# Attention on one core: one comparison row moved from VectorE to ScalarE, a subtraction moved from GpSimd to VectorE, GpSimd's sums at another place, and TensorE's loop written out

## The chip, the cores and the metric

The kernel runs on one core of a Trainium2 chip. The metric is the device time of one execution in microseconds (us). The core's engines work side by side and meet at semaphores: TensorE (PE in the profile; its weight loads are PEld), VectorE (DVE), ScalarE (ACT), GpSimd (POOL) and SyncE (SP), which here only issues DMAs.

## The reference

`x` is 2048 rows of 512 numbers, `adj` a 2048 x 2048 matrix of zeros and ones. A graph attention layer with 16 heads of 32 columns is followed by an expert layer; the change touches the first alone.

```python
seq = (layernorm(x) @ W_seq).reshape(N, H, DH)          # N = 2048, H = 16, DH = 32
scores = score1[:, :, None] + score2[:, None, :]        # seq . a1 and seq . a2, for each head
scores = leaky_relu(scores, 0.2)
scores = scores + (1.0 - adj)[None, :, :] * MASK_VAL    # -65500
attn = softmax(scores, axis=-1)
hidden = einsum('hij,jhd->ihd', attn, seq).reshape(N, 512)
x = x + elu(hidden @ W_out + b_out)
x = x + expert_layer(layernorm(x))
```

## The kernel before, in words

The exponential of a leaky ReLU of a sum is one of two products, chosen by the sign of score1 + score2. So the kernel builds no softmax matrix. For each head it builds a matrix of zeros and ones, "is the sum positive", masks it with `adj`, and multiplies it with a value matrix that holds both products for each of the 2048 columns; a second matrix product with `adj` itself supplies the part of the other sign. Both are scaled for each row and added.

**Units.** The work is cut into 32 units: 8 pairs of heads `p`, and in each pair four units `k` = 0 to 3, where `k // 2` is the head of the pair and `k % 2` the half of the 2048 output rows (1024 of them). I number units u = 4p + k, from 0 to 31. A unit's mask matrix `m8[:, k]` has 16 rows (blocks `j` of 128 columns of the reference's matrix), each of 128 partitions x 1024 bytes. `DVE_J` of the 16 rows are compared on VectorE (`compare`, L653), the others on ScalarE by a steep sigmoid (`compare_rows`, L600). VectorE then masks its own rows (`mask_own`, L661) and those of ScalarE (`mask_acts`, L668) with a bitwise and.

**The value matrix.** `vs[:, b]` holds one head's values as two float16 halves, a high and a low one, whose sum stands for a float32. GpSimd forms four products in `vtmp` (L735 twice, L737 twice), ScalarE rounds them to the high half (`split_high`, L608), and GpSimd subtracts to get the low half (L741). There is one `vtmp`.

**Matmuls.** TensorE runs 256 matmuls for a unit (L791 with 132 columns, L795 with 66), into three PSUM banks; the units alternate between two sets of banks. It starts unit u when its masks are ready (`m_ready`), when the low half is there (`lo_ready`, at even k), and when the sums of unit u-2 have been read out (`sums_ready`).

**VectorE's loop.** The iteration for unit u (28 of them, for u = 0 to 27, in a hardware loop over p) waits until TensorE has finished unit u, reads its sums out of PSUM in three reductions (`collect`, L675), compares the rows of unit u+4, masks its own rows of unit u+4, and masks ScalarE's rows of unit u+3. For the last four units only `collect` is left (and one `mask_acts`).

**ScalarE's loop.** When unit u is done it compares its rows of unit u+4; at odd k it first does `split_high` for the next pair.

**GpSimd's loop.** `combine` (L750 twice, L755) scales and adds the sums of unit u as soon as `collect` of u is done; at odd k `build` comes ahead of it: the four products, the wait for ScalarE, the subtraction.

SyncE stages the score rows of unit u+2 by DMA when both compares of unit u are done (L558). All loops over p are hardware loops, TensorE's too (L778).

Of the kernel before, what the change touches and what calls it, by code (L numbers as in the profile page):

```python
# [30 lines left out]
ALU = mybir.AluOpType  # L31
# [11 lines left out]
WD = 2 * W1  # L43
# [4 lines left out]
MB = 4  # L48
AB = 3
UNITS = H * NIC  # L50
DVE_J = 7
E, LAT, INTER, SH = 8, 256, 256, 2048
TC = 512
NC_ = N // TC
# [12 lines left out]
def build(nc, x, adjT, w_seq, a_cols, a_mask, w_out, b_out, gateT, corr, w1T, w2T, fc1T, fc2T, upT, downT,  # L67
# [6 lines left out]
    with ctx:  # L74
        def sem(name):
            return ctx.enter_context(nc.semaphore(name))
# [34 lines left out]
        vs = at(O_VS, 2112, f16).rearrange("p (b j c) -> p b j c", b=2, j=T)  # L111
# [429 lines left out]


        PAIRS = H // 2
        prod_ready, hi_copied, lo_ready, vtmp_free = sem("prod_ready"), sem("hi_copied"), sem("lo_ready"), sem("vtmp_free")
        dve_compared, act_compared, own_masked = sem("dve_compared"), sem("act_compared"), sem("own_masked")
        m_ready, unit_in_psum, sums_ready, sums_free = sem("m_ready"), sem("unit_in_psum"), sem("sums_ready"), sem("sums_free")
        act_passed, pe_passed = sem("act_passed"), sem("pe_passed")
        bias_copied, scaled_step = sem("bias_copied"), sem("scaled_step")

        GROUPS = [(0, 3), (3, 3), (6, 2)]  # L550
# [2 lines left out]
        with nc.Block() as block:  # L553
# [93 lines left out]
            def _(dve):  # L647
# [23 lines left out]
                def collect(p, k):  # L671
# [5 lines left out]
                            bank[3 * (k % 2) + g][:, 0:n * WV].rearrange("p (t s c) -> p t c s", t=n, s=2), AX.X)  # L677
                    last.then_inc(sums_ready, 1)

                def split_low():  # L680

                    dve.wait_ge(wo_high, 1)
                    nc.vector.tensor_tensor(wo_parts[:, 1, :, :], wo_sb, wo_parts[:, 0, :, :].bitcast(f32), ALU.subtract)
                    nc.vector.tensor_tensor(bout_parts[0:1, 1, :], bout_sb[0:1, :], bout_parts[0:1, 0, :].bitcast(f32),
                                            ALU.subtract)
                    nc.vector.tensor_scalar(ones_r[0:1, :], ident2[0:1, :], 0.0, 1.0, ALU.mult, ALU.add).then_inc(wo_low, 1)

                def body(p, last):
                    for k in range(4):
                        if last and k == 3:  # L690
                            split_low()
                        dve.wait_ge(unit_in_psum, 4 * p + k + 1)
                        collect(p, k)
                        if not last:
                            compare(p + 1, k)
                            mask_own(p + 1, k)

                        if k == 0:
                            mask_acts(p, 3)
                        elif not last:  # L700
                            mask_acts(p + 1, k - 1)
# [10 lines left out]
                apply_empty_rows((2, 3))  # L712
                dve.wait_ge(seq_in_psum, T)
                compare(0, 1)
                mask_own(0, 1)
                mask_acts(0, 1)
                compare(0, 2)
                mask_own(0, 2)
                compare(0, 3)
# [6 lines left out]
            @block.gpsimd  # L726
            def _(pool):
                setup_pool(pool)
                def build(p, b):

                    h = 2 * p + b
                    pool.wait_ge(vtmp_free, 2 * p + b + 1)
                    vh = v_sb.rearrange("p t (h d) -> p t h d", h=H)[:, :, h, :]
                    for c, val in enumerate((bval, nval)):
                        nc.gpsimd.tensor_tensor(vtmp[:, :, c * W1:c * W1 + DH], vh,  # L735
                                                val[:, :, bass.ds(h, 1)].to_broadcast([P, T, DH]), ALU.mult)
                        last = nc.gpsimd.tensor_copy(vtmp[:, :, c * W1 + DH:(c + 1) * W1], val[:, :, bass.ds(h, 1)])  # L737
                    last.then_inc(prod_ready, 1)
                    pool.wait_ge(prod_ready, 2 * p + b + 1)
                    pool.wait_ge(hi_copied, 2 * p + b + 1)  # L740
                    nc.gpsimd.tensor_tensor(vs[:, b, :, WD:], vtmp, vs[:, b, :, 0:WD], ALU.subtract).then_inc(lo_ready, 1)  # L741
                    pool.wait_ge(lo_ready, 2 * p + b + 1)
                    pool.sem_inc(vtmp_free, 1)

                def combine(p, k):
                    h = 2 * p + k // 2
# [8 lines left out]
                    nc.gpsimd.tensor_tensor(hid[:, tiles, h, :], scaled[:, k % 2, :, 0:W1],  # L755
                                            scaled[:, k % 2, :, W1:], ALU.add).then_inc(sums_free, 1)

                def body(p, last):
                    for k in range(4):
                        if k % 2 and not last:  # L760
                            pool.wait_ge(unit_in_psum, 4 * p + k + 1)
                            build(p + 1, k // 2)
                        combine(p, k)

                pool.sem_inc(sums_free, 2)
                pool.sem_inc(vtmp_free, 1)
                pool.wait_ge(bn_ready, 1)
                pool.wait_ge(v_copied, T)
                build(0, 0)
                build(0, 1)  # L770
                with pool.Fori(0, PAIRS - 1) as p:
                    body(p, False)
                body(PAIRS - 1, True)

            @block.tensor
            def _(pe):
                setup_pe(pe)
                with pe.Fori(0, PAIRS) as p:  # L778
                    for k in range(4):
                        b = k // 2  # L780
                        if k % 2 == 0:
                            pe.wait_ge(lo_ready, 2 * p + b + 1)
                        pe.wait_ge(sums_ready, 4 * p + k + 1)
                        pe.wait_ge(m_ready, 4 * p + k + 1)
                        pe.sem_inc(pe_passed, 1)
                        for i in range(IT):
                            g, slot = GROUP_OF[i]
                            o = bank[3 * (k % 2) + g][:, slot * WV:(slot + 1) * WV]
# [1010 lines left out]
```

## Time and profile before

| | us |
|---|---|
| three timed runs: median (lowest to highest) | 1131.07 (1130.83 to 1133.75) |
| the profiled execution: its own time | 1135.76 |
| its span, first to last instruction | 1133.9 |
| VectorE busy | 856.1 (75%) |
| TensorE busy | 1042.5 (92%) |
| ScalarE busy | 618.2 (55%) |
| GpSimd busy | 315.0 (28%) |

The stage that the change touches runs from about 110 us to 565 us of the span. Matmuls overlap, so TensorE's busy time isn't its work; starts of groups of matmuls say more. In a row of the timeline the first number is the start, the second the duration; rows of one kind are merged with their count.

### The profile page before, as it was taken

How to read it: one execution, taken by the hardware profiler on the slowest of the kernel's cores; microseconds unless marked ns; L12 is line 12 of the kernel's file. 1: busy time of each engine (PE TensorE's matmuls, PEld its weight loads, DVE VectorE, ACT ScalarE, POOL GpSimd, SP SyncE). 2: the span in 40 equal slices, each digit the busy share in tenths (PEclk: the TensorE clock that was granted, in tenths of full speed). 3: DMA queues.
4: the chain of work that ended last, by engine and by line, in shares of the span. 5: the costliest groups of instructions: out<-in, count | busy, mean ns of one | idle time of the engine just before them, and what ended most of it. 6: DMA issues, size and time to landing. Idle time of an engine off the chain costs nothing. (4 is left out here: it accounts for less than half of the span.)

```text
span 1133.9 us, 27344 instructions
## 1 busy us (share of the span) xinstructions
PE 1042.5 (92%) x11304; PEld 916.3 (81%) x11304; DVE 856.1 (75%) x1216; ACT 618.2 (55%) x939; POOL 315.0 (28%) x287
## 2 busy tenths in 40 slices
PE   5799687989898989978899999999999999999998
PEld 4576587989898989978867788888888887777887
DVE  4756999999999999997359953345876558985554
ACT  2226777777777777773045543334445445664432
POOL 1101434444444445463234200000026300005510
PEclk9899898999898989898989999999999999999999
DMA  8356011111111111153073510002016213444242
GB/s 299 112 192 240 20 58 40 40 40 40 40 46 52 40 40 40 40 168 113 2 285 123 174 58 1 1 1 75 1 48 212 85 42 126 131 130 150 75 141 101
DMA packets 51472, 102.68 MB, mean 91 GB/s; under 512 B 5889, under 2 KB 25985, under 8 KB 48770
## 3 DMA queue, kind: packets, MB, share of 16 engines
q1 hardware_dynamic: 44386, 81.68, 21.2%
q10 hardware_dynamic: 3888, 10.72, 2.6%
q0 software_dynamic: 3072, 8.39, 2.3%
q8 instruction: 105, 1.72, 0.6%
q14 instruction: 21, 0.17, 0.1%
HBM read 74.69 MB, written 26.08 MB: 89 GB/s over the span
## 5 line engine op out<-in xcount | busy, mean ns | idle before, releaser
L791 PE MATMUL bank<-arena 128*128 128x132 f16 x4096 | 298.0, 226 | 52.6 <-issue 43.3
L600 ACT ACTIVATE arena<-arena 128x1024 fp8e4<-128x1024 f32 x288 | 303.2, 1135 | 7.4 <-DMA arena<-s_rows 4.5
L791 PEld LDWEIGHTS bank<-arena 128*128 128x128 fp8e4 x4096 | 256.1, 100 | 56.8 <-issue 56.8
L653 DVE TENSOR_SCALAR arena<-arena 128x1024 uint8<-128x1024 f32 x224 | 205.9, 988 | 0.0
L1170 PE MATMUL bank<-xt,up_parts 128*128 128x512 f32 x768 | 186.3, 391 | 0.0
L1637 PE MATMUL bank<-down_parts,h_parts 128*128 128x512 f32 x768 | 184.5, 389 | 0.1
L795 PE MATMUL bank<-arena 128*128 128x66 f16 x4096 | 179.3, 199 | 0.0
L1637 PEld LDWEIGHTS bank<-down_parts,h_parts 128*128 128x128 f32 x768 | 144.0, 188 | 30.5 <-issue 0.5
L1170 PEld LDWEIGHTS bank<-xt,up_parts 128*128 128x128 f32 x768 | 142.3, 188 | 28.7 <-ACT relu_sb L1119 0.2
L795 PEld LDWEIGHTS bank<-arena 128*128 128x128 fp8e4 x4096 | 160.8, 100 | 0.0
L1144 DVE TENSOR_TENSOR relu_sb<-relu_sb 128x512 f32<-128x512 f32 x64 | 44.3, 692 | 116.9 <-ACT relu_sb L1119 111.7
L750 POOL TENSOR_TENSOR arena<-arena 128x264 f32<-128x264 f32 x64 | 65.2, 1038 | 220.4 <-DVE arena L675 219.6
L1119 ACT ACTIVATE relu_sb<-bank 128x512 f32<-128x512 f32 x64 | 38.3, 598 | 147.3 <-PE bank L1170 140.9
L668 DVE TENSOR_TENSOR arena<-arena 128x2304 uint32<-128x2304 uint32 x32 | 105.5, 3298 | 0.2
L1591 POOL DMA_INDIRECT sorted_latent_rows<-latent,slot_idx x32 | 35.0, 1094 | 208.7 <-DVE slot_idx L1457 190.9
L1159 DVE TENSOR_TENSOR down_parts<-down_sb,down_parts 128x512 fp32r<-128x512 f32 x64 | 44.3, 691 | 51.3 <-ACT down_parts L1138 47.8
L1138 ACT CAST down_parts<-down_sb 128x512 fp32r<-128x512 f32 x64 | 39.9, 623 | 73.8 <-PE bank L1637 70.5
L1603 POOL DMA_INDIRECT y_gathered<-sorted_expert_rows,slot_idx x32 | 32.9, 1028 | 154.5 <-DMA sorted_expert_rows<-expert_y 133.9
L661 DVE TENSOR_TENSOR arena<-arena 128x1792 uint32<-128x1792 uint32 x32 | 67.2, 2101 | 1.1
L608 ACT CAST arena<-arena 128x1056 f16<-128x1056 f32 x16 | 17.2, 1074 | 89.9 <-POOL arena L737 89.9
L675 DVE TENSOR_REDUCE arena<-bank 128x198 f32<-128x396 f32 (+1 forms) x96 | 44.1, 513 | 24.0 <-PE bank L791 24.0
L735 POOL TENSOR_TENSOR arena<-arena 128x512 f32 (+1 forms) x32 | 47.7, 1490 | 28.3 <-ACT arena L209 25.1
(225 smaller groups left out, 1477.8 us busy)
## 6 DMA issues: line engine op xcount, KB each, us to landing
hid<-in_adjT SPq DMA_DIRECT2D x16, 1024.0 KB, 4.9
arena<-s_rows SPq DMA_DIRECT2D x30, 512.0 KB, 3.8
sorted_latent_rows<-zeros SPq DMA_DIRECT2D x1, 4992.0 KB, 18.7
xs<-sorted_latent_rows SPq DMA_DIRECT2D x39, 128.0 KB, 2.2
sorted_expert_rows<-expert_y SPq DMA_DIRECT2D x39, 128.0 KB, 1.7
arena<-in_x SPq DMA_DIRECT2D x4, 1024.0 KB, 12.0
xr<-in_x SPq DMA_DIRECT2D x16, 256.0 KB, 2.8
up_sb<-in_upT ACTq DMA_DIRECT2D x1, 4096.0 KB, 14.7
```

The costliest lines, as they stand in the source:

```text
L600: last = nc.scalar.activation(m8[:, k, j, :], s1b[:, k % 2, :], ACT.Sigmoid, bias=bias_now[:, k // 2, j:j + 1], scale=STEEP, saturate=False)
L653: last = nc.vector.tensor_scalar(mu8[:, k, j, :], s1b[:, k % 2, :], neg_s2[:, 2 * p + k // 2, j:j + 1], float(ONE8), ALU.is_gt, ALU.mult)
L661: nc.vector.tensor_tensor(mw[:, k, 0:DVE_J, :], mw[:, k, 0:DVE_J, :], adjw[:, 0:DVE_J, cols], ALU.bitwise_and).then_inc(own_masked, 1)
L668: nc.vector.tensor_tensor(mw[:, k, DVE_J:, :], mw[:, k, DVE_J:, :], adjw[:, DVE_J:, cols], ALU.bitwise_and).then_inc(m_ready, 1)
L735: nc.gpsimd.tensor_tensor(vtmp[:, :, c * W1:c * W1 + DH], vh, val[:, :, bass.ds(h, 1)].to_broadcast([P, T, DH]), ALU.mult)
L750: last = nc.gpsimd.tensor_tensor(scaled[:, k % 2, :, c * W1:(c + 1) * W1], sums[:, k % 2, :, c * W1:(c + 1) * W1], coef[:, h, tiles, c:c + ...
L791: last = nc.tensor.matmul(o, m8[:, k, j, i * P:(i + 1) * P], vs[:, b, j, :], start=(j == 0), stop=(j == T - 1))
L795: nc.tensor.matmul(od, adj8[:, ja, (k % 2) * IC + i * P:(k % 2) * IC + (i + 1) * P], vs[:, b, ja, :].rearrange("p (s c) -> p s c", s=2)[:, ...
L1144: nc.vector.tensor_tensor(r, r, r, ALU.mult).then_inc(sq_ready, 1)
L1159: nc.vector.tensor_tensor(sb_[:, s % 2, 1, :], down_sb[:, s % FS, :], sb_[:, s % 2, 0, :].bitcast(f32), ALU.subtract).then_inc(b_ready, 1)
L1170: last = nc.tensor.matmul(bank[6 + s % 2][:, :], sa[:, s % 2, a, k, :], xt[c][:, b, k, :], start=(i == 0), stop=(i == len(mm) - 1))
L1637: last = nc.tensor.matmul(ob[t][:, :], hhl[:, s % 2, a, t * P:(t + 1) * P], sb_[:, s % 2, b, :], start=(n == 0 and (a, b) == TERMS[0]), st ...
```

## The change

It does four things.

- `DVE_J` goes from 7 to 6: VectorE compares 6 rows of each unit and ScalarE 10. `mask_own` shrinks from 1792 to 1536 words a partition and `mask_acts` grows from 2304 to 2560.
- The subtraction that gives the low half moves from GpSimd to VectorE (`low_values`), behind the compare at odd k; GpSimd keeps the four products (`products`).
- GpSimd handles unit u-1 (`combine`) in the iteration for u, when `m_ready` has reached u+3 (the last thing in VectorE's iteration before) and TensorE has finished u. The products move from odd k to even k, behind `combine`, with a wait for the low half of the head before. The semaphore `vtmp_free` goes.
- TensorE's loop over the 8 pairs is written out.

```diff
-DVE_J = 7
+DVE_J = 6
@@ VectorE
+                def low_values(p, b):
+                    dve.wait_ge(hi_copied, 2 * p + b + 1)
+                    nc.vector.tensor_tensor(vs[:, b, :, WD:], vtmp, vs[:, b, :, 0:WD], ALU.subtract).then_inc(lo_ready, 1)
...
                             compare(p + 1, k)
+                            if k % 2:
+                                low_values(p + 1, k // 2)
                             mask_own(p + 1, k)
...
                 compare(0, 1)
+                low_values(0, 0)
                 mask_own(0, 1)
                 mask_acts(0, 1)
+                low_values(0, 1)
                 compare(0, 2)
@@ GpSimd
-                def build(p, b):
+                def products(p, b):
...
-                    pool.wait_ge(vtmp_free, 2 * p + b + 1)
...
                     last.then_inc(prod_ready, 1)
-                    pool.wait_ge(prod_ready, 2 * p + b + 1)
-                    pool.wait_ge(hi_copied, 2 * p + b + 1)
-                    nc.gpsimd.tensor_tensor(vs[:, b, :, WD:], vtmp, vs[:, b, :, 0:WD], ALU.subtract).then_inc(lo_ready, 1)
-                    pool.wait_ge(lo_ready, 2 * p + b + 1)
-                    pool.sem_inc(vtmp_free, 1)
...
-                def body(p, last):
+                def body(p, first):
                     for k in range(4):
-                        if k % 2 and not last:
-                            pool.wait_ge(unit_in_psum, 4 * p + k + 1)
-                            build(p + 1, k // 2)
-                        combine(p, k)
+                        pool.wait_ge(m_ready, 4 * p + k + 3)
+                        pool.wait_ge(unit_in_psum, 4 * p + k + 1)
+                        if k or not first:
+                            combine(p - (k == 0), (k - 1) % 4)
+                        if k % 2 == 0:
+                            pool.wait_ge(lo_ready, 2 * (p + 1) + k // 2)
+                            products(p + 1, k // 2)
...
-                build(0, 0)
-                build(0, 1)
-                with pool.Fori(0, PAIRS - 1) as p:
+                products(0, 0)
+                pool.wait_ge(lo_ready, 1)
+                products(0, 1)
+                body(0, True)
+                with pool.Fori(1, PAIRS - 1) as p:
                     body(p, False)
-                body(PAIRS - 1, True)
+                combine(PAIRS - 2, 3)
+                for k in range(4):
+                    combine(PAIRS - 1, k)
@@ TensorE
-                with pe.Fori(0, PAIRS) as p:
+                for p in range(PAIRS):
```

**VectorE, ahead of its loop.** The rows are the last work before the first `collect`; L682 is `low_values`, and `hi_copied` is what ScalarE's `split_high` raises.

```order
 L653 TENSOR_SCALAR arena<-arena 128x1024 [waits s1_staged_hi,seq_in_psum,dve_step]
-L653 TENSOR_SCALAR arena<-arena 128x1024 x6
-L661 TENSOR_TENSOR arena<-arena 128x1792 [waits dve_compared]
-L668 TENSOR_TENSOR arena<-arena 128x2304 [waits own_masked,act_compared]
+L653 TENSOR_SCALAR arena<-arena 128x1024 x5
+L682 TENSOR_TENSOR arena<-arena 128x16x66 [waits hi_copied]
+L661 TENSOR_TENSOR arena<-arena 128x1536 [waits dve_compared]
+L668 TENSOR_TENSOR arena<-arena 128x2560 [waits own_masked,act_compared]
+L682 TENSOR_TENSOR arena<-arena 128x16x66 [waits hi_copied]
 L653 TENSOR_SCALAR arena<-arena 128x1024 [waits s1_staged_lo]
```

The two subtractions of the first pair of heads now stand in VectorE's queue, the second one ahead of the compare of unit 2.

**VectorE, an iteration at odd k in its loop.** The rows run from the last reduction of `collect` to the mask of ScalarE's rows.

```order
 L675 TENSOR_REDUCE arena<-bank 128x132
 L653 TENSOR_SCALAR arena<-arena 128x1024 [waits s1_staged_hi]
-L653 TENSOR_SCALAR arena<-arena 128x1024 x6
+L653 TENSOR_SCALAR arena<-arena 128x1024 x5
+L681 REGISTER_ALU
+L682 TENSOR_TENSOR arena<-arena 128x16x66 [waits hi_copied]
 L660 REGISTER_ALU
-L661 TENSOR_TENSOR arena<-arena 128x1792 [waits dve_compared]
-L668 TENSOR_TENSOR arena<-arena 128x2304 [waits own_masked,act_compared]
```

One comparison is gone and one subtraction of 16 x 66 elements has come, between the compare and `mask_own`.

**GpSimd, in its loop.** First the kernel before, from the products of one head to the `combine` behind them.

```order
-L732 REGISTER_ALU [waits unit_in_psum]
-L735 ISA [waits vtmp_free]
-L735 REGISTER_ALU
-L735 TENSOR_TENSOR arena<-arena 128x16x32
-L737 COPY arena<-arena 128x16
-L735 ISA
-L735 TENSOR_TENSOR arena<-arena 128x16x32
-L737 COPY arena<-arena 128x16
-L741 TENSOR_TENSOR arena<-arena 128x16x66 [waits hi_copied,prod_ready]
-L748 REGISTER_ALU [waits lo_ready]
-L750 ISA [waits sums_ready]
```

Now the changed kernel, where `combine` is L752 and L757, and the products are L742 and L744.

```order
+L752 ISA [waits sums_ready,unit_in_psum,m_ready]
+L752 TENSOR_TENSOR arena<-arena 128x8x33
+L752 ISA
+L752 TENSOR_TENSOR arena<-arena 128x8x33
+L757 ISA [waits scaled_step]
+L757 TENSOR_TENSOR hid<-arena 128x8x33
+L767 REGISTER_ALU
+L742 ISA [waits lo_ready]
+L742 REGISTER_ALU
+L742 TENSOR_TENSOR arena<-arena 128x16x32
+L744 COPY arena<-arena 128x16
```

The wait for ScalarE in the middle of GpSimd's work is gone, and `combine` stands ahead of the products behind a wait for VectorE's last mask.

## Rows read from the trace of the kernel before

**Rows 1.** Windows: VectorE's 28 iterations, then the tail; PEclk is the granted clock.

```profile
155.37:527.93 372.56, 332.29 (x6921) 328.90 (x6922) 371.60 (x338) 273.33 (x273) 178.22 (x154) 0.93 0.16 53
528.00:562.00 34.00, 34.00 (x759) 34.00 (x756) 10.37 (x14) 2.42 (x2) 10.32 (x9) 1.00 0.16 52
```

**Rows 2.** Timeline of VectorE over two iterations in the middle of its loop.

```profile
304.53 1.37 DVE L675 TENSOR_REDUCE arena<-bank 128x198 f32<-128x396 f32 x3
305.82 5.88 DVE L653 TENSOR_SCALAR arena<-arena 128x1024 uint8<-128x1024 f32 x7
...
313.68 2.55 DVE L668 TENSOR_TENSOR arena<-arena 128x2304 uint32<-128x2304 uint32 x1
316.14 1.38 DVE L675 TENSOR_REDUCE arena<-bank 128x198 f32<-128x396 f32 x3
317.44 7.51 DVE L653 TENSOR_SCALAR arena<-arena 128x1024 uint8<-128x1024 f32 x7
324.99 2.02 DVE L661 TENSOR_TENSOR arena<-arena 128x1792 uint32<-128x1792 uint32 x1
326.93 4.46 DVE L668 TENSOR_TENSOR arena<-arena 128x2304 uint32<-128x2304 uint32 x1
331.32 1.37 DVE L675 TENSOR_REDUCE arena<-bank 128x198 f32<-128x396 f32 x3
```

**Rows 3.** Timeline of GpSimd over the same stretch.

```profile
306.09 2.02 POOL L750 TENSOR_TENSOR arena<-arena 128x264 f32<-128x264 f32 x2 [3.90 <-DVE arena L675]
...
317.74 1.99 POOL L750 TENSOR_TENSOR arena<-arena 128x264 f32<-128x264 f32 x2 [8.57 <-DVE arena L675]
...
326.35 2.63 POOL L741 TENSOR_TENSOR arena<-arena 128x1056 f16<-128x1056 f32 x1 [1.33 <-ACT arena L608]
```

**Rows 4.** Timeline of VectorE ahead of its loop.

```profile
113.37 3.35 DVE L397 TENSOR_TENSOR arena<-arena 128x2048 uint32<-128x2048 uint32 x1
...
123.69 2.29 DVE L397 TENSOR_TENSOR arena<-arena 128x2048 uint32<-128x2048 uint32 x1
...
130.13 4.73 DVE L653 TENSOR_SCALAR arena<-arena 128x1024 uint8<-128x1024 f32 x7
...
155.37 1.38 DVE L675 TENSOR_REDUCE arena<-bank 128x198 f32<-128x396 f32 x3
```

**Rows 5.** Timeline, 435 to 438 us: a GpSimd subtraction beside `collect`.

```profile
435.53 3.06 POOL L741 TENSOR_TENSOR arena<-arena 128x1056 f16<-128x1056 f32 x1 [1.33 <-ACT arena L608]
436.54 1.37 DVE L675 TENSOR_REDUCE arena<-bank 128x198 f32<-128x396 f32 x3
```

**Rows 6.** Timeline of GpSimd in the tail, where VectorE is idle.

```profile
540.81 1.24 POOL L750 TENSOR_TENSOR arena<-arena 128x264 f32<-128x264 f32 x2 [7.22 <-DVE arena L675]
```

**Rows 7.** Timeline of ScalarE: split, nine compares, and the copy of the biases.

```profile
325.12 1.07 ACT L608 CAST arena<-arena 128x1056 f16<-128x1056 f32 x1 [6.22 <-POOL arena L737]
326.10 9.46 ACT L600 ACTIVATE arena<-arena 128x1024 fp8e4<-128x1024 f32 x9
335.46 0.19 ACT L592 COPY arena<-arena 128x16 f32 x1
```

**Rows 8.** Waits, 85 to 560 us: total, times, longest.

```profile
ACT arena L608 <- POOL arena L737: 89.9, 16, 7.2
PEld bank L791 <- issue: 56.8, 22, 6.9
```

**Rows 9.** Timeline of TensorE: start of unit 0, then of unit 28 with a second stall.

```profile
123.15 0.27 PE L791 MATMUL bank<-arena 128*128 128x132 f16 x1 [6.47 <-issue]
...
509.95 0.27 PE L791 MATMUL bank<-arena 128*128 128x132 f16 x1 [5.82 <-issue]
...
516.03 0.73 PE L791 MATMUL bank<-arena 128*128 128x132 f16 x5 [3.69 <-issue]
```

**Rows 10.** Timeline of VectorE: `collect` of unit 28 and of unit 31.

```profile
527.93 1.38 DVE L675 TENSOR_REDUCE arena<-bank 128x198 f32<-128x396 f32 x3
...
562.38 1.39 DVE L675 TENSOR_REDUCE arena<-bank 128x198 f32<-128x396 f32 x3 [6.31 <-PE bank L791]
```

More of the change, by code:

```diff
@@ L543, in build @@
         PAIRS = H // 2
-        prod_ready, hi_copied, lo_ready, vtmp_free = sem("prod_ready"), sem("hi_copied"), sem("lo_ready"), sem("vtmp_free")
+        prod_ready, hi_copied, lo_ready = sem("prod_ready"), sem("hi_copied"), sem("lo_ready")
         dve_compared, act_compared, own_masked = sem("dve_compared"), sem("act_compared"), sem("own_masked")
         m_ready, unit_in_psum, sums_ready, sums_free = sem("m_ready"), sem("unit_in_psum"), sem("sums_ready"), sem("sums_free")
-        act_passed, pe_passed = sem("act_passed"), sem("pe_passed")
+        act_passed = sem("act_passed")
         bias_copied, scaled_step = sem("bias_copied"), sem("scaled_step")
@@ L756, in combine @@
                                             scaled[:, k % 2, :, W1:], ALU.add).then_inc(sums_free, 1)
-                def body(p, last):
+                def body(p, first):
                     for k in range(4):
-                        if k % 2 and not last:
-                            pool.wait_ge(unit_in_psum, 4 * p + k + 1)
-                            build(p + 1, k // 2)
-                        combine(p, k)
+                        pool.wait_ge(m_ready, 4 * p + k + 3)
[5 more added lines that the diff above has]
+                            products(p + 1, k // 2)
                 pool.sem_inc(sums_free, 2)
-                pool.sem_inc(vtmp_free, 1)
                 pool.wait_ge(bn_ready, 1)
                 pool.wait_ge(v_copied, T)
-                build(0, 0)
-                build(0, 1)
-                with pool.Fori(0, PAIRS - 1) as p:
+                products(0, 0)
[3 more added lines that the diff above has]
+                with pool.Fori(1, PAIRS - 1) as p:
                     body(p, False)
-                body(PAIRS - 1, True)
+                combine(PAIRS - 2, 3)
+                for k in range(4):
+                    combine(PAIRS - 1, k)
             @block.tensor
@@ L784, in _ @@
                         pe.wait_ge(m_ready, 4 * p + k + 1)
-                        pe.sem_inc(pe_passed, 1)
                         for i in range(IT):
```

## The prediction

> **What bounds the kernel now.** I read the windows first, to find the engine without idle time. Over VectorE's 28 iterations, 155.4 to 527.9 us, it is busy 371.6 of 372.6 us; ScalarE is busy 273, GpSimd 178 [rows 1]. TensorE shows 332, but its matmuls overlap. Its real need is read where nothing holds it up: in the tail it runs 759 matmuls in 34.0 us, so a unit of 256 takes 11.5 us [rows 1]. The loop takes 372.6 / 28 = 13.3 us a unit. So VectorE sets the pace there, and TensorE is 1.8 us a unit ahead of it.
>
> The timeline of VectorE shows what a unit costs. Two neighbouring iterations take 11.6 us (304.5 to 316.1) and 15.2 us (316.1 to 331.3), 26.8 for both [rows 2]. They do the same work. The difference is in two places: the seven compares take 5.88 us in the one and 7.51 in the other, and the mask of ScalarE's rows 2.55 and 4.46. The timeline of GpSimd says why [rows 3]: in both, `combine` starts right behind `collect`, beside the compares; in the second the four products follow it; and the 2.63 us subtraction (326.35) lies on the slow mask. Ahead of the loop, where GpSimd is idle, the same seven compares take 4.73 us [rows 4]. So GpSimd's work costs VectorE 1.15 us for each `combine` (5.88 - 4.73), 1.63 for a head's products (7.51 - 5.88), and 1.91 for the subtraction: 5.84 in two iterations of 26.8.
>
> After the last compare the bound changes. From the `collect` of unit 28 to that of unit 31 there are 34.45 us [rows 10], three units of TensorE at 11.5. TensorE should have been further ahead, since two sets of banks let it be. But it started unit 28 at 509.95 after 5.8 us without a releaser and stood still again for 3.7 us [rows 9]. Such stalls sum to 56.8 us in 22 places [rows 8]; the large ones that I show follow the loop's jump back.
>
> **The change, part by part.**
>
> *VectorE's own work.* I count from start to start, without GpSimd, for two iterations. `collect` is 1.30 (316.14 to 317.44) [rows 2]. A compare row is 4.73 / 7 = 0.68, so six are 4.1. `mask_own` is 1.94 to the next start for 1792 words; between 2.02 us for 1792 and 2.55 for 2304 lies 1.03 ns a word [rows 2], so 1536 words are 1.68. `mask_acts` goes from 2.47 to 2.73. That is 9.8 us an iteration. `low_values` has no row on VectorE. By the same 1.03 ns an element, 1056 elements cost about 1.2 us; the bounds are nothing and GpSimd's 2.63 for the same subtraction [rows 3]. I take 1.2, because VectorE's own two-input rows are nearest. It comes in one iteration of two: 20.8 us for two iterations, where the old work alone is 21.0. So one compare is traded for half a subtraction, and almost the whole gain must come from the other 5.84 us.
>
> *GpSimd beside VectorE.* The 1.91 of the subtraction goes. `combine` now starts with `collect`, not behind it. Does it cost anything there? Once in the trace a GpSimd subtraction (435.53 to 438.6) lies right over a `collect`, which took 1.37 us, as everywhere [rows 5]. So a `combine` in that place costs nothing. Alone, its first two operations take 1.24 us [rows 6], about the 1.30 of `collect`; the third falls on the compares, a third of 1.15, 0.39. The products stay beside the compares: 1.63 for two iterations. Together 1.63 + 2 x 0.39 = 2.4, and 0.14 for a late start of GpSimd, since its sequencer has register work first (my estimate). Two iterations cost 20.8 + 2.5 = 23.3 us, or 11.65 a unit. If nothing of `combine` were hidden, it would be 20.8 + 1.63 + 2.3 = 24.7, or 12.35 a unit.
>
> The Trainium skill ("SBUF — State Buffer", Who interferes with whom) has `tensor_reduce` never in contention with GpSimd, and the trace agrees (1.37 us). The same section calls the shared port pair an exclusive lock, held for the whole instruction. By that rule VectorE would lose the full time of each GpSimd operation, some 12.2 us a unit and 15 us more in all by my estimate; the trace doesn't agree, since a `combine` of 1.9 us alone costs 1.15.
>
> *The other engines at that pace.* ScalarE's nine compares take 9.36 us from start to start; ten take 10.4, and two units with one split (0.98) and the copy of the biases with its wait (0.4) 22.2 us, or 11.1 a unit [rows 7]. Today the split waits on GpSimd's products, 89.9 us in 16 times [rows 8], because both start at the same signal. Now the products are made one iteration earlier, so ScalarE finds them. TensorE needs 11.5. So three engines stand at 11.1, 11.5 and 11.65. VectorE remains the last, by little; as TensorE may be up to two units ahead, unequal iterations even out.
>
> *TensorE's loop written out* removes the jumps. In the loop VectorE's 1.8 us a unit hid their stalls; now that cover is 0.15 us, so this edit is what lets the others count. It gains by itself only in the tail. There, `collect` of unit 28 is followed by 1.4 us and two units of 11.5, 24.4 us to the `collect` of unit 31 instead of 34.45: -10.0.
>
> *The start.* This is the one place that gets worse. TensorE started unit 0 at 123.15 [rows 9]. Now the low half of head 0 comes from VectorE, behind the compare of unit 1 that started at 130.13 [rows 4]. With GpSimd idle the instructions ahead of it shorten: one `L397` took 3.35 beside GpSimd and 2.29 alone, and I count four such pieces, 3.7 us with the missing compare not counted. So the compare starts at 126.4, the low half is ready at 126.4 + 4.1 + 1.2 = 131.7, and TensorE starts 8.5 us later. It has slack: VectorE wants unit 1 only in its second iteration. What is queued behind VectorE's second `low_values` matters more: GpSimd's products of head 1 begin at 131.7 and take some 7 us beside the masks, ScalarE's split is done at about 139.7, the low half at 140.9. Then VectorE has two compares, two `mask_own` and one `mask_acts`, 14.3 us, and reaches its first `collect` at 155.2, where it is now (155.37). ScalarE, held at that same split, has its rows of unit 3 at about 161; VectorE wants them at about 163. I add 0.5 us for a wait for the second split.
>
> *The sum.* The 28 iterations: 28 x 11.65 = 326.2 for 372.6, -46.4. Start: -0.2 + 0.5. Tail: -10.0. Total -56 us. The profiled execution took 1135.8 us, for a span of 1133.9, so the same execution would take 1079.7. The median of the timed runs is 4.7 below that execution, so by it 1075. I say 1077. The expert layer behind is started by TensorE's and VectorE's last unit and moves as a whole.
>
> **The rivals.**
>
> *GpSimd's cost stays, or the clock does.* If `combine` isn't hidden, or starts late, 12.35 a unit instead of 11.65 is 28 x 0.7 = 20 us: 1097. The clock gives the same sum. In the loop the mean granted clock is 0.93 of 2.4 GHz, 1.00 in the tail [rows 1]. If short gaps between units kept it at 0.93, a unit would take 11.5 / 0.93 = 12.4. Against it: with 0.15 us of idle a unit there should be hardly a gap.
>
> *TensorE stalls in straight code too.* Without the first, the stalls are some 50 us for 28 units [rows 8], 1.8 a unit. If they belonged to the amount of instructions and not to the jump, TensorE would need 11.5 + 1.8 = 13.3 us and nothing would be gained: 1131. Against it speaks that 34 us of the tail went without one [rows 1]. The Trainium skill ("Runtime: NRT & Kernel Launch", Instruction fetch mechanics) says that a taken branch breaks the sequential prefetch; the stall at 509.95, at the top of the loop's body, agrees.
>
> *Slower: ScalarE becomes the bound.* It has 1.1 us to spare in two units. If GpSimd, now behind two more waits, made the products late for the split, ScalarE would wait there, VectorE's `low_values` with it, and everything behind that in VectorE's queue. At the longest wait of today, 7.2 us [rows 8], two units cost 29.4: 14 x 2.6 = 36 us more, 10 less in the tail, 1157. It beats the old 26.8 from a wait of 4.6 us on. Against it: the products have a whole iteration.
>
> *TensorE is the bound.* Should VectorE need under 11.5, the unit stays there: 28 x 0.15 = 4 us less, 1073, and with a better start a few more.
>
> **How the numbers follow.** The forecast (1067 to 1090) has 0.64, GpSimd's cost or the clock (1091 to 1104) 0.24, TensorE at its bound with a start so much better that it ends below 1067 0.04, stalls in straight code 0.05, ScalarE 0.03. A price of 2.63 for `low_values` would give 28 x 0.7 = 20 us more, 1097 too. The range of 1066 to 1100 leaves out somewhat under 2 in 10. A difference of 0.3%, 3.4 us, is about what a measurement of this kernel tells from none. Faster 0.92, same 0.05, slower 0.03.
>
> **What the changed profile would show.** The start of one `collect` to the one after the next should be 23.3 us, with compares of 4.1 to 4.5 us at odd k and about 6.1 at even k, `mask_acts` never above 2.9, `low_values` 1.2 to 1.3. TensorE should start unit 0 near 131.7 and show no stalls at the heads of pairs. The first `collect` should start near 155 and the last near 506. I am wrong if six compares still take over 5.2 us at odd k, if the split waits for GpSimd in the loop, or if TensorE has idle time without a releaser.

## The result and the profile after

The changed kernel takes 1078.18 us (median of four runs, 1076.02 to 1079.98) where the kernel before takes 1132.41 (1130.83 to 1133.92). The ratio is 0.9525, with a 95% interval of 0.9501 to 0.9548: 4.75% faster, 54 us. The prediction was 1077.

The profiled execution of the changed kernel took 1076.02 us for a span of 1074.2. Its windows over VectorE's 28 iterations and over the tail answer to [rows 1]; the columns are the same.

```profile
152.90:479.68 326.78, 324.60 (x7174) 322.67 (x7170) 325.20 (x323) 313.84 (x314) 119.16 (x140) 1.00 0.20 67
480.00:505.00 25.00, 25.00 (x556) 25.00 (x554) 10.29 (x13) 2.42 (x2) 10.54 (x9) 1.00 0.01 3
```

The 28 iterations take 326.8 us instead of 372.6, or 11.67 a unit. VectorE is still busy all the time, but now TensorE and ScalarE are too: 325, 325 and 314 us of 327. The granted clock is 1.00 where it was 0.93. The timeline of VectorE over two iterations answers to [rows 2].

```profile
269.13 1.38 DVE L675 TENSOR_REDUCE arena<-bank 128x198 f32<-128x396 f32 x3
270.43 6.09 DVE L653 TENSOR_SCALAR arena<-arena 128x1024 uint8<-128x1024 f32 x6
276.55 1.76 DVE L661 TENSOR_TENSOR arena<-arena 128x1536 uint32<-128x1536 uint32 x1
278.23 2.82 DVE L668 TENSOR_TENSOR arena<-arena 128x2560 uint32<-128x2560 uint32 x1
280.96 1.38 DVE L675 TENSOR_REDUCE arena<-bank 128x198 f32<-128x396 f32 x3
282.26 4.50 DVE L653 TENSOR_SCALAR arena<-arena 128x1024 uint8<-128x1024 f32 x6
286.67 1.25 DVE L682 TENSOR_TENSOR arena<-arena 128x1056 f16<-128x1056 f32 x1
287.84 1.75 DVE L661 TENSOR_TENSOR arena<-arena 128x1536 uint32<-128x1536 uint32 x1
289.51 2.82 DVE L668 TENSOR_TENSOR arena<-arena 128x2560 uint32<-128x2560 uint32 x1
```

From 269.13 to 280.96 to 292.25 are 11.83 and 11.29 us, 23.1 for both; the two iterations behind them take 23.5, and 23.3 is the mean. In the loop the masks are 1.76 and 2.82 everywhere, with nothing beside them. Only the compares still vary, 6.09 with GpSimd's products and 4.50 without; in every second pair of iterations they are 6.30 and 4.63. There `combine` starts 0.46 and 0.42 us behind the start of `collect`, not 0.26 and 0.30, and its second operation reaches further into the compares. GpSimd's timeline over the same stretch answers to [rows 3].

```profile
269.39 1.24 POOL L752 TENSOR_TENSOR arena<-arena 128x264 f32<-128x264 f32 x2 [8.95 <-DVE arena L668]
270.81 0.87 POOL L757 TENSOR_TENSOR hid<-arena 128x264 f32 x1 [0.18 <-POOL arena L752]
271.64 1.52 POOL L742 TENSOR_TENSOR arena<-arena 128x512 f32 x1
273.11 0.67 POOL L744 COPY arena<-arena 128x16 f32 x1
```

The first two operations of `combine` lie beside `collect`, at the 1.24 us that they take alone [rows 6], and `collect` keeps its 1.38 us. They were 2.02 beside the compares.

Ahead of the loop, the timeline of VectorE answers to [rows 4]; the second row is `low_values` of head 0, the fourth that of head 1, the last that of head 2 in the second iteration, and a bracket is the idle time ahead.

```profile
107.74 0.69 DVE L395 TENSOR_SCALAR arena<-bank 128x512 uint8<-128x512 f32 x1 [5.01 <-PE bank L460]
...
128.53 1.25 DVE L682 TENSOR_TENSOR arena<-arena 128x1056 f16<-128x1056 f32 x1
...
131.55 3.51 DVE L668 TENSOR_TENSOR arena<-arena 128x2560 uint32<-128x2560 uint32 x1
137.45 1.26 DVE L682 TENSOR_TENSOR arena<-arena 128x1056 f16<-128x1056 f32 x1 [2.39 <-ACT arena L608]
...
144.39 4.06 DVE L653 TENSOR_SCALAR arena<-arena 128x1024 uint8<-128x1024 f32 x6
...
152.90 1.38 DVE L675 TENSOR_REDUCE arena<-bank 128x198 f32<-128x396 f32 x3
...
170.38 1.26 DVE L682 TENSOR_TENSOR arena<-arena 128x1056 f16<-128x1056 f32 x1 [1.10 <-ACT arena L608]
```

TensorE starts unit 0 right behind the first `low_values`, later than in [rows 9], and the `collect` of units 28 and 31 stand at 479.68 and 505.33 where [rows 10] had them at 527.93 and 562.38. First TensorE's timeline, then VectorE's.

```profile
129.83 0.29 PE L798 MATMUL bank<-arena 128*128 128x132 f16 x1 [15.01 <-DVE arena L682]
...
476.82 0.24 PE L802 MATMUL bank<-arena 128*128 128x66 f16 x2 [0.54 <-issue]
```

```profile
479.68 1.37 DVE L675 TENSOR_REDUCE arena<-bank 128x198 f32<-128x396 f32 x3
...
505.33 1.39 DVE L675 TENSOR_REDUCE arena<-bank 128x198 f32<-128x396 f32 x3 [6.31 <-PE bank L798]
```

### The profile page after: what moved, and what is told of

Read it like the earlier page. It is cut to its first block, busy times and chain, and to the rows that moved or that the text cites. A ratio compares the mean times of both kernels' runs of the same rounds, so it can differ in the third digit from the quotient of the medians.

```text
span 1074.2 us, 27252 instructions
## 1 busy us (share of the span) xinstructions
PE 1018.5 (95%) x11304; PEld 894.5 (83%) x11304; DVE 806.5 (75%) x1200; ACT 648.9 (60%) x971; POOL 247.7 (23%) x271
## 4 chain that ended last, share of the span: by engine, by line
PE 47%; DVE 2%; issue 2%; DMA 1%; POOL 0%; ACT 0%; SPq 0%; POOLq 0%; DVEq 0%; ACTq 0%
PE bank L1177 16%; PE bank L1644 16%; PE bank L1009 3%; PE bank L1721 2%; PE bank L1672 1%; PE bank L1673 1%; PE bank L1675 1%; DMA xs<-sorted_latent_rows 1%; PE bank L1691 1%; PE bank L1665 1%; PE bank L1629 1%; PE bank L1006 1%; PE bank L1627 1%; PE bank L997 1%; PE bank L1018 1%
## 5 line engine op out<-in xcount | busy, mean ns | idle before, releaser
L600 ACT ACTIVATE arena<-arena 128x1024 fp8e4<-128x1024 f32 x320 | 336.4, 1135 | 3.0 <-ACT arena L592 3.0
L798 PE MATMUL bank<-arena 128*128 128x132 f16 x4096 | 283.8, 221 | 15.6 <-DVE arena L682 15.0
L798 PEld LDWEIGHTS bank<-arena 128*128 128x128 fp8e4 x4096 | 245.0, 97 | 17.7 <-DVE arena L682 15.5
L802 PE MATMUL bank<-arena 128*128 128x66 f16 x4096 | 172.6, 195 | 1.6 <-issue 1.6
L653 DVE TENSOR_SCALAR arena<-arena 128x1024 uint8<-128x1024 f32 x192 | 166.4, 933 | 0.0
L802 PEld LDWEIGHTS bank<-arena 128*128 128x128 fp8e4 x4096 | 153.7, 98 | 1.9 <-issue 1.9
L752 POOL TENSOR_TENSOR arena<-arena 128x264 f32<-128x264 f32 x64 | 45.4, 731 | 218.9 <-DVE arena L668 195.9
L668 DVE TENSOR_TENSOR arena<-arena 128x2560 uint32<-128x2560 uint32 x32 | 90.8, 2838 | 0.2
L1598 POOL DMA_INDIRECT sorted_latent_rows<-latent,slot_idx x32 | 34.7, 1085 | 209.0 <-DVE slot_idx L1464 191.0
L742 POOL TENSOR_TENSOR arena<-arena 128x512 f32 (+1 forms) x32 | 48.6, 1520 | 63.2 <-ACT arena L209 25.1
L661 DVE TENSOR_TENSOR arena<-arena 128x1536 uint32<-128x1536 uint32 x32 | 56.1, 1753 | 0.6
L1009 PE MATMUL bank<-wo_parts,hT 128*128 128x512 f32 x192 | 49.7, 409 | 0.0
```

Source lines behind the costliest of these rows:

```text
L600: last = nc.scalar.activation(m8[:, k, j, :], s1b[:, k % 2, :], ACT.Sigmoid, bias=bias_now[:, k // 2, j:j + 1], scale=STEEP, saturate=False)
L653: last = nc.vector.tensor_scalar(mu8[:, k, j, :], s1b[:, k % 2, :], neg_s2[:, 2 * p + k // 2, j:j + 1], float(ONE8), ALU.is_gt, ALU.mult)
L661: nc.vector.tensor_tensor(mw[:, k, 0:DVE_J, :], mw[:, k, 0:DVE_J, :], adjw[:, 0:DVE_J, cols], ALU.bitwise_and).then_inc(own_masked, 1)
L668: nc.vector.tensor_tensor(mw[:, k, DVE_J:, :], mw[:, k, DVE_J:, :], adjw[:, DVE_J:, cols], ALU.bitwise_and).then_inc(m_ready, 1)
L752: last = nc.gpsimd.tensor_tensor(scaled[:, k % 2, :, c * W1:(c + 1) * W1], sums[:, k % 2, :, c * W1:(c + 1) * W1], coef[:, h, tiles, c:c + ...
L798: last = nc.tensor.matmul(o, m8[:, k, j, i * P:(i + 1) * P], vs[:, b, j, :], start=(j == 0), stop=(j == T - 1))
```

## The experiments

Eight kernels were run, and the changed one again as a reference. Ratios are to the kernel before, measured on the same chip. The first three undo one part of the change each, the fourth does one part alone.

### TensorE's loop as a hardware loop again

```diff
-                for p in range(PAIRS):
+                with pe.Fori(0, PAIRS) as p:
...
                         pe.wait_ge(m_ready, 4 * p + k + 1)
+                        pe.sem_inc(pe_passed, 1)
```

The semaphore increment stood in the loop of the kernel before too, and went with it. It stands ahead of all four units of a turn.

> The changed kernel with TensorE's loop over the head pairs as a hardware loop again (and its semaphore increment before each unit). Theory: the stalls behind each jump cost TensorE about 1.8 us a unit, and now nothing covers them, so a unit takes 11.5 + 1.8 = 13.3 us instead of 11.65, 28 units give +46 us, and the stall at unit 28 another 10: 1078 becomes about 1125 to 1134, nearly the whole gain gone. Rival A: writing out the loop is worth only the tail's 10 us, 1088. Rival B: VectorE's waits cover part of the stalls in the loop, as its own pace is 11.65: 1100 to 1115.

Measured: 1126.0 us, ratio 0.9952 (0.9935 to 0.9969). Of 54 us only 6 are left. TensorE's timeline in this kernel shows the start of the loop's body in two neighbouring turns.

```profile
394.47 0.22 PE L799 MATMUL bank<-arena 128*128 128x132 f16 x1 [2.78 <-DVE arena L675]
397.02 0.73 PE L799 MATMUL bank<-arena 128*128 128x132 f16 x5 [1.19 <-issue]
446.47 0.22 PE L799 MATMUL bank<-arena 128*128 128x132 f16 x1 [3.14 <-issue]
449.50 0.73 PE L799 MATMUL bank<-arena 128*128 128x132 f16 x5 [1.56 <-issue]
```

The bracket of the first row names VectorE, that of the third, at the same place one turn later, nobody. Such gaps stand in the first unit of a turn alone, not at its other three, so they belong to the jump and not to the increment. VectorE's waits in this kernel show who is late:

```profile
DVE arena L675 <- PE bank L799: 60.3, 9, 10.1
```

VectorE, almost without idle time in the loop of both main kernels, waits 60.3 us in nine places for TensorE: six are at the head of a turn, three in the tail, where the changed kernel waits too. This turn is 52 us (394.5 to 446.5), 13.0 a unit. So the stalls of the jump are real time for TensorE, some 6 us a turn with the lower granted clock (0.93 over the loop, where the changed kernel has 1.00), and the first theory stands, with 1.5 us a unit and not the 1.8 that it took. Rivals A and B fall.

### `combine` behind its own `collect` again

```diff
                     for k in range(4):
-                        pool.wait_ge(m_ready, 4 * p + k + 3)
-                        pool.wait_ge(unit_in_psum, 4 * p + k + 1)
-                        if k or not first:
-                            combine(p - (k == 0), (k - 1) % 4)
+                        combine(p, k)
                         if k % 2 == 0:
```

> The changed kernel with GpSimd's combine of unit u right behind collect of unit u again, in the same iteration (products still at even k behind it). Theory: three GpSimd operations lie beside the compares and cost VectorE 1.15 us an iteration instead of about 0.45: 28 x 0.7 = +20 us, 1098, with six compares at odd k near 5.2 us. Rival: the place doesn't matter, because TensorE at 11.5 us a unit is nearly the bound and collect loses as much as the compares gain: 1078 within 4 us.

Measured: 1096.02 us, ratio 0.9681 (0.9654 to 0.9708): 18 us more than the changed kernel. VectorE's timeline:

```profile
301.12 6.04 DVE L653 TENSOR_SCALAR arena<-arena 128x1024 uint8<-128x1024 f32 x6
307.19 2.51 DVE L661 TENSOR_TENSOR arena<-arena 128x1536 uint32<-128x1536 uint32 x1
...
313.68 5.21 DVE L653 TENSOR_SCALAR arena<-arena 128x1024 uint8<-128x1024 f32 x6
```

At odd k the compares take 5.21 us, as said; at even k the work that no longer fits beside them has moved on to `mask_own`, 2.51 instead of 1.76. Two iterations take 24.5 us (299.83 to 324.38). That is 0.6 us an iteration for three operations beside the compares instead of one.

### The subtraction on GpSimd again, beside the compares

```diff
                         if k % 2 == 0:
                             pool.wait_ge(lo_ready, 2 * (p + 1) + k // 2)
                             products(p + 1, k // 2)
+                        else:
+                            low_pool(p + 1, k // 2)
@@ VectorE
-                            if k % 2:
-                                low_values(p + 1, k // 2)
```

> The changed kernel with the subtraction of the low half on GpSimd again, but behind combine at odd k, so beside the compares and mask_own and not on mask_acts. Theory (what matters is which VectorE instruction GpSimd's work lies on): two iterations lose VectorE's 1.2 us and gain 0.4 to 1.9 us of collisions, a difference of -0.8 to +0.7 us for two iterations, 14 x that is -11 to +10 us, but TensorE's 11.5 us a unit lets no more than 4 us be gained: 1074 to 1088. The nearest row for a collision with compares says 0.4 us for each us of GpSimd, 2.63 us give 1.05: 1076. Rival (the move to VectorE is itself the gain, since the subtraction costs 1.9 us wherever it stands on GpSimd): 1088. TensorE starts unit 0 some 9 us earlier, which should not show in the end.

Measured: 1087.64 us, ratio 0.9607 (0.9582 to 0.9631): 9.5 us more than the changed kernel. Here the theory falls and the rival holds. The timelines of VectorE and of GpSimd at odd k:

```profile
333.55 6.36 DVE L653 TENSOR_SCALAR arena<-arena 128x1024 uint8<-128x1024 f32 x6
```

```profile
310.03 0.87 POOL L753 TENSOR_TENSOR hid<-arena 128x264 f32 x1 [0.19 <-POOL arena L748]
310.87 2.56 POOL L759 TENSOR_TENSOR arena<-arena 128x1056 f16<-128x1056 f32 x1
```

Six compares take 6.36 us beside the subtraction and 4.50 without: it costs VectorE 1.86 us, as it did on the mask (1.91), and not the 1.05 that I had worked out from `combine`. On VectorE itself it adds 1.05: in the changed kernel, with GpSimd idle, the compares and `low_values` take 5.15 us up to `mask_own` (124.54 to 129.69), the compares alone 4.10 (144.39 to 148.49). The difference of 0.81 us is 11.3 over 14 pairs of iterations, and VectorE's wait of 1.1 us in the second iteration (170.38) is gone. That makes 10.2, and the 28 iterations of the two profiles differ by 10.3 (337.05 and 326.78). TensorE started unit 0 at 123.18 here, 6.6 us earlier than in the changed kernel, and had to wait for VectorE all the same.

### The kernel before, with TensorE's loop written out

```diff
-                with pe.Fori(0, PAIRS) as p:
+                for p in range(PAIRS):
```

> The kernel before with TensorE's loop written out and nothing else. Theory: in the loop VectorE sets the pace at 13.3 us a unit and hides TensorE's stalls, so only the tail gains: 10 us, 1122 for 1132. Rival: TensorE's stalls held VectorE up somewhere too, or its lower clock did: more than 15 us gained, below 1117.

Measured: 1128.72 us, ratio 0.9963 (0.9948 to 0.9978): 3 us gained (2 to 6 by the interval), fewer than the 10 expected, and the rival is out. The tail did shrink: from the `collect` of unit 28 to that of unit 31 it is 25.1 us (530.80 to 555.90) instead of 34.45. But the 28 iterations ahead of it are longer, 375.2 us instead of 372.6. In the kernel before TensorE's stalls had twice shifted GpSimd's products, so that the subtraction began behind the start of the mask, and not ahead of it. VectorE's timeline of the kernel before at one such place, then of this one at the same place:

```profile
434.06 2.56 DVE L668 TENSOR_TENSOR arena<-arena 128x2304 uint32<-128x2304 uint32 x1
```

```profile
434.40 4.47 DVE L668 TENSOR_TENSOR arena<-arena 128x2304 uint32<-128x2304 uint32 x1
```

In the kernel before, the subtraction ran from 435.53 [rows 5], on the end of the mask and over `collect`, and the two iterations took 25.4 us (423.33 to 448.75). Without the stalls all pairs of iterations take 26.8. So over a quarter of the tail's gain, 2.6 of 9.4 us, was given back in the loop. That leaves 6.8 us of gain by the two traces, where the medians differ by 3.2; why stays open.

### Seven rows, and five, on VectorE

```diff
-DVE_J = 6
+DVE_J = 7
```

> The changed kernel with seven compare rows of a unit on VectorE and nine on ScalarE, as before the change. Theory: VectorE is the last of three engines by 0.15 us a unit, so one more row of 0.68 us counts in full: 28 x 0.68 = +19 us, 1097. Rival: TensorE or ScalarE really sets the pace at 11.6 us and part of the row is hidden: less than 12 us more, under 1090.

Measured: 1099.97 us, ratio 0.9697 (0.9675 to 0.972). By the ratios, 0.9697 against 0.9525, it is 19.5 us slower than the changed kernel. VectorE's two iterations take 24.4 and 24.8 us in turn, 24.6 in the mean, where 23.3 + 2 x 0.68 = 24.7 was expected. The row counts in full. With five rows:

```diff
-DVE_J = 6
+DVE_J = 5
```

> The changed kernel with five compare rows on VectorE and eleven on ScalarE. Theory: ScalarE needs 22.2 us for two units and 1.04 us more for each row, 24.3, so 12.15 us a unit, above TensorE's 11.5 and VectorE's 11.0; ScalarE sets the pace and VectorE waits at the mask of ScalarE's rows: 28 x 0.5 = +14 us, 1092. Rival: ScalarE's slack between its units is more than I read, and TensorE's 11.5 is the floor: 1074.

Measured: 1095.28 us, ratio 0.9664 (0.9648 to 0.968), by the ratios 15.7 us slower than the changed kernel. ScalarE's timeline:

```profile
295.00 1.06 ACT L608 CAST arena<-arena 128x1056 f16<-128x1056 f32 x1
295.97 11.54 ACT L600 ACTIVATE arena<-arena 128x1024 fp8e4<-128x1024 f32 x11
307.41 0.19 ACT L592 COPY arena<-arena 128x16 f32 x1
307.81 11.55 ACT L600 ACTIVATE arena<-arena 128x1024 fp8e4<-128x1024 f32 x11 [0.21 <-ACT arena L592]
319.27 1.06 ACT L608 CAST arena<-arena 128x1056 f16<-128x1056 f32 x1
```

No idle time but the 0.21 of the bias copy, and 24.3 us from split to split (295.00 to 319.27), as expected. VectorE waits, though not where I had said: it waits at `low_values` for the split, 34.7 us in 15 places, and at the mask of ScalarE's rows only 6.7 us in three.

```profile
DVE arena L682 <- ACT arena L608: 34.7, 15, 4.6
```

So of five, six and seven rows six is the best number, and both sides fall off at once.

### An earlier first low half, and two copies on ScalarE

These were measured side by side with the changed kernel.

> The changed kernel unchanged, as the reference for the two kernels beside it: 1078.

Measured: 1079.23 us (1078.08 to 1080.19), ratio 0.9537 (0.9522 to 0.9552).

```diff
                 apply_empty_rows((0, 1))
+                low_values(0, 0)
                 mask_own(0, 0)
...
                 compare(0, 1)
-                low_values(0, 0)
                 mask_own(0, 1)
```

> The changed kernel with VectorE's first low_values (head 0) ahead of the first mask_own, not behind the compare of unit 1. Theory: GpSimd can form the products of head 1 some 14 us earlier, ScalarE's split no longer leaves VectorE waiting for 2.4 us ahead of its loop and 1.1 us in its second iteration, and GpSimd's products then lie on VectorE's masks and cost it up to 2 us: 1.5 to 3.5 us gained, 1075 to 1076.5. TensorE starts unit 0 near 118 instead of 129.8. Rival: TensorE's late start is what the changed kernel pays at its beginning: then 8 us or more would be gained, below 1070. Rival: VectorE's collisions eat the gain: 1078.

Measured: 1075.24 us (1074.36 to 1076.17), ratio 0.9498 (0.9484 to 0.9512). That is 4.0 us less than the changed kernel beside it, with no run of the one among the runs of the other. Both waits for the split are gone, as its timeline of VectorE shows.

```profile
109.91 0.69 DVE L395 TENSOR_SCALAR arena<-bank 128x512 uint8<-128x512 f32 x1 [5.30 <-PE bank L460]
...
137.59 1.25 DVE L682 TENSOR_TENSOR arena<-arena 128x1056 f16<-128x1056 f32 x1
...
153.03 1.38 DVE L675 TENSOR_REDUCE arena<-bank 128x198 f32<-128x396 f32 x3
...
169.32 1.25 DVE L682 TENSOR_TENSOR arena<-arena 128x1056 f16<-128x1056 f32 x1
```

From the first row to the first `collect` are 43.1 us; in the reference beside it 45.2 (108.20 to 153.36), and its second iteration has another 1.1 us of waiting. TensorE starts unit 0 at 122.7, not near 118, since it needs unit 0's masks as well; it then waits for VectorE twice more (1.45 and 5.01 us), so its start isn't what counts. The theory holds, but the 4.0 us are a little more than the 1.5 to 3.5 that it gave; the start of the two profiles gives 2.0 of them, the loop 1.2 and the tail 0.2.

```diff
                     for c, val in enumerate((bval, nval)):
-                        nc.gpsimd.tensor_tensor(vtmp[:, :, c * W1:c * W1 + DH], vh,
+                        last = nc.gpsimd.tensor_tensor(vtmp[:, :, c * W1:c * W1 + DH], vh,
                                                 val[:, :, bass.ds(h, 1)].to_broadcast([P, T, DH]), ALU.mult)
-                        last = nc.gpsimd.tensor_copy(vtmp[:, :, c * W1 + DH:(c + 1) * W1], val[:, :, bass.ds(h, 1)])
@@ ScalarE, split_high
+                    for c, val in enumerate((bval, nval)):
+                        last = nc.scalar.copy(vtmp[:, :, c * W1 + DH:(c + 1) * W1], val[:, :, bass.ds(h, 1)])
+                    last.then_inc(cols_copied, 1)
+                    act.wait_ge(cols_copied, 2 * p + b + 1)
```

> The kernel beside it (early low half) and the two copies of 16 columns of each head's products moved from GpSimd to ScalarE, just ahead of its split. Theory: GpSimd loses two of four operations beside the compares of even k, VectorE gains up to 0.8 us in two units (23.3 to 22.5), TensorE with 11.5 us a unit becomes the bound: 28 x 0.13 = 4 us more gained than beside it, 1071 to 1073. Rival: ScalarE, with 22.2 + 0.6 us for two units, comes too near to 23.0 and its delays reach VectorE's masks: no gain over the kernel beside it, or a loss of a few us.

Measured: 1075.31 us (1072.78 to 1076.27), ratio 0.9498 (0.9481 to 0.9515): the same as the kernel beside it. Neither the theory nor the rival explains it. ScalarE isn't late, and the compares haven't changed; VectorE's and GpSimd's timelines:

```profile
315.63 6.09 DVE L658 TENSOR_SCALAR arena<-arena 128x1024 uint8<-128x1024 f32 x6
```

```profile
314.58 1.24 POOL L756 TENSOR_TENSOR arena<-arena 128x264 f32<-128x264 f32 x2 [8.95 <-DVE arena L673]
...
316.83 3.01 POOL L747 TENSOR_TENSOR arena<-arena 128x512 f32 x2
```

The six compares take 6.09 us with the copies on GpSimd and 6.09 without. So the copies of 16 columns cost VectorE nothing; the two products cost it everything, 1.59 us. ScalarE still waits for them ahead of its split, 0.58 us at 320.02, and VectorE doesn't wait for ScalarE.

## Why the prediction was right, step by step

**VectorE's own work.** Right. `low_values` takes 1.25 us, 1.17 to the next start, and adds 1.05, where I took 1.2; six compares alone take 4.07, the masks 1.76 and 2.82.

**GpSimd beside VectorE.** Right for this kernel. `collect` loses nothing to `combine`; what is left of it costs 4.50 - 4.06 = 0.44 us (0.39 said), the products 6.09 - 4.50 = 1.59 (1.63 said). The other pairs of iterations cost 0.34 more by the late start of `combine`, 0.17 in the mean, where I had guessed 0.14. Two iterations take 23.3 us as said. The second experiment shows the gain of the placement by itself: 18 us. What I didn't foresee is what the cost hangs on. In the third expectation I took it by GpSimd's time in the trace and was off by nearly half; see the last section. By the third experiment the move of the subtraction from GpSimd is worth 9.5 us against a place beside the compares.

**The other engines.** ScalarE needs 22.2 us for two units, with no wait for the products: from 258.01 to 280.18 are 22.17.

```profile
258.01 1.06 ACT L608 CAST arena<-arena 128x1056 f16<-128x1056 f32 x1
...
280.18 1.06 ACT L608 CAST arena<-arena 128x1056 f16<-128x1056 f32 x1
```

As it is faster than VectorE's 23.3, it runs ahead until it meets GpSimd's products. From 369 us on each split waits for them, 0.2 to 1.0 us in five places, 4.2 in all. I had named this as a sign of being wrong. It was a bad sign to name: VectorE waits for a split only twice, at 137.45 and 170.38, so these waits cost nothing.

The other two signs showed as well, once or briefly. The six compares of the last iteration, at odd k, take 5.65 us (468.53), since the `combine` behind GpSimd's loop doesn't wait for VectorE's mask and lies on them too. And TensorE has 1.6 us without a releaser in three places, from 463 to 477.

Experiments five and six show that VectorE and ScalarE really stand within a row of each other.

**TensorE's loop.** Right that it "is what lets the others count": alone it gives 3 us, the other three parts alone 6 (the first experiment), all four 54. But the 1.8 us a unit of [rows 8] were no price of the stalls. A TensorE that needs 11.5 us where VectorE takes 13.3 is idle for 1.8 in any case. The same view of the fourth kernel, whose loop is written out, still has almost all of it:

```profile
PEld bank L791 <- issue: 49.4, 17, 7.1
```

That the stalls cost 1.5 by the first experiment, near to 1.8, is luck. No term of the sum rested on it; the rival of stalls in straight code did. The tail's term was a little too large. It takes 25.65 us (479.68 to 505.33), where I had 24.4, which I put down to short stalls, one of them shown above, that are left in the straight code just ahead of it.

**The start.** Right. This execution reached the first `L395` at 107.74, where the kernel before had it at 109.6, 1.85 us earlier for reasons ahead of the change. With that taken off, I had TensorE at 129.85 and the first `collect` at 153.35; they are at 129.83 and 152.90. The wait in the loop for which I had put 0.5 us was 1.1 (170.38).

**The sum.** 372.6 to 326.8 in the iterations is -45.8 (-46.4 said, +0.5 for the wait); the tail -8.8 (-10.0 said). From last `collect` to last `collect` the profiles differ by 57.05 us, of which 1.85 belong to the setup. The profiled executions differ by 59.7 us and the medians by 54, since the one of before lies 3.4 us above its median and the one of after 2.2 below. Of the 59.7, 2.65 lie behind the last `collect`. That part differs between executions of one kernel: in the two profiles of the changed kernel it is 568.9 and 571.7 us, while the stretch from the first `L395` to the last `collect` is 397.6 and 397.4. So that stretch gained 55.2 us, where I had said 56. That 1077 came within 1.2 us of 1078.18 is in part luck.

**The rivals.** Clock: what gaps there are didn't lower it; the granted clock is 1.00 over the loop. It is 1.00 too in the kernel of the second experiment, with gaps of 0.36 and 0.82 us ahead of its units (window 152.90 to 479.68). Straight code: 1.6 us of stalls in three places. ScalarE as the bound: only with a row more.

## What to carry to other kernels

When GpSimd shares a stage with a saturated VectorE, price each of its operations by what it takes from VectorE (see below), and put it beside VectorE's reads of PSUM; a `combine` moved by half an iteration was worth 18 us here. Parts of such a change don't add: with three engines within 5% of each other, an edit is worth little alone (3 and 6 us) and much when the next engine in line is freed too (54 us). And before writing off a stall as hidden, ask how much cover it will have when the bound has moved: 1.8 us a unit of cover were 0.15 afterwards.

## What the hardware showed beyond expectation

**What GpSimd takes from VectorE is priced by the time of its operation alone, not by its time beside the compares.** Beside the compares one operation of 264 elements cost VectorE 0.44 us, two of 512 cost 1.59, one of 1056 cost 1.86, and copies of 16 elements nothing. In the trace these operations take 0.87, 1.52, 2.56 and 0.67 us, but alone they take less. The timeline of the changed kernel has all but the subtraction alone, the first two rows ahead of VectorE's stage and the last in the tail.

```profile
106.09 1.07 POOL L742 TENSOR_TENSOR arena<-arena 128x512 f32<-128x512 f32 x1 [25.10 <-ACT arena L209]
107.11 0.21 POOL L744 COPY arena<-arena 128x16 f32<-128x16 f32 x1
...
508.11 0.64 POOL L757 TENSOR_TENSOR hid<-arena 128x264 f32<-128x264 f32 x1
```

The subtraction has about 2.05 by the kernel before, from the end of `mask_own` to its own end (326.93 to 328.98, [rows 2] and [rows 3]). So each operation cost VectorE 0.2 to 0.3 us less than its time alone: 0.20, 0.27, 0.19, and the copy has only 0.21 to lose. The three operations of `combine` beside the compares fit too, 1.88 alone and 1.15 lost. This is an estimate from these rows. A price by elements, 1.45 to 1.8 ns each, fits nearly as well, and nothing was run to part the two. I had scaled by GpSimd's time in the trace, which made the subtraction too cheap, 1.05 us for 1.86.

On a mask it matters who starts first. The subtraction that began 0.6 us ahead of the mask cost it 1.91 us ([rows 2] and [rows 3]). Where GpSimd began behind the start of a mask, the mask kept its time and GpSimd waited, as in the kernel before at the end of the loop, in VectorE's and GpSimd's timelines.

```profile
529.22 2.55 DVE L668 TENSOR_TENSOR arena<-arena 128x2304 uint32<-128x2304 uint32 x1
```

```profile
529.39 3.48 POOL L750 TENSOR_TENSOR arena<-arena 128x264 f32<-128x264 f32 x2 [8.44 <-DVE arena L675]
```

GpSimd's two operations take 1.24 alone [rows 6]. The Trainium skill ("SBUF — State Buffer", Who interferes with whom) calls the shared port an exclusive lock for the whole instruction. These rows agree with it, better than I said in the prediction: on the masks within 0.2 us, beside the compares short of it by up to 0.3 us an operation. Where these 0.3 us come from, no run here shows.

**A stall on one engine can save time on another.** TensorE's stalls in the kernel before had twice moved a GpSimd subtraction from ahead of VectorE's mask to behind its start, which saved 1.2 and 1.4 us (25.6 and 25.4 for 26.8).
